# One-hot matrices of a table look-up: a compare per chunk of table rows with one row number per partition, in place of one compare of two tensors per piece

## The reference

```python
e = jnp.stack([tbl_0[ids[:, 0]], ..., tbl_26[ids[:, 26]]], axis=1)      # [2048, 27, 128]
dot_products = jnp.einsum('bnd,bmd->bnm', e, e)
z = dot_products[:, c, r]                                               # r, c = np.tril_indices(27, k=-1)
h = jnp.concatenate([z.reshape(2048, -1), dense_ctx], axis=1)           # 351 + 16
h = jnp.maximum(h @ W_top1 + b_top1, 0.0)                               # 512
h = jnp.maximum(h @ W_top2 + b_top2, 0.0)                               # 256
y = h @ W_top3                                                          # 1
```

## Time and profile before

| | us |
|---|---|
| median of 3 executions | 354.51 (354.46 to 360.79) |
| the profiled execution, its own time | 354.21 |
| span that its trace covers | 352.1 |
| TensorE busy | 330.7 (94%) |
| VectorE busy | 250.9 (71%) |
| GpSimd busy | 244.4 (69%) |
| ScalarE busy | 148.8 (42%) |

### The profile page before, as it was taken

One profiled execution on the slowest core, in us unless ns is written; L12 is line 12 of the kernel. 1 busy time (PEld: TensorE's weight loads), 2 busy tenths in 40 slices (PEclk: granted clock), 3 DMA queues, 4 the chain that ended last, 5 costly groups with the idle time before them and its releaser, 6 DMA issues.

```text
span 352.1 us, 12745 instructions
## 1 busy us (share of the span) xinstructions
PE 330.7 (94%) x5664; PEld 278.9 (79%) x5664; DVE 250.9 (71%) x335; ACT 148.8 (42%) x304; POOL 244.4 (69%) x265
## 2 busy tenths in 40 slices
PE   1897879999999999999999999999999999999986
PEld 0686768888888888888888888888888888887775
DVE  3899999989839696587929698487938786420322
ACT  2256543443534254433644245442545246535321
POOL 5777776777777777777777777777777777777100
PEclk9999999999999999999999999999999999999999
DMA  7997574443433433243332433243342332222000
GB/s 219 323 270 244 128 217 104 99 116 92 122 85 90 108 85 103 55 119 85 90 94 77 107 99 80 77 114 85 89 98 59 83 95 71 57 57 59 20 4 3
DMA packets 21928, 36.81 MB, mean 105 GB/s; under 512 B 7907, under 2 KB 12003, under 8 KB 21874
## 3 DMA queue, kind: packets, MB, share of 16 engines
q0 software_dynamic: 8256, 16.92, 19.7%
q1 hardware_dynamic: 13474, 18.55, 18.0%
q10 hardware_dynamic: 144, 0.52, 0.4%
HBM read 35.97 MB, written 0.01 MB: 102 GB/s over the span
## 4 chain that ended last, share of the span: by engine, by line
PE 87%; DVE 8%; issue 2%; DMA 1%; ACT 1%; SPq 0%; DVEq 0%
PE e_banks L560 42%; PE g_banks L594 13%; PE w_banks L624 10%; PE e_banks L572 9%; PE w_banks L655 8%; DVE one_hot L781 5%; DVE table_lo L762 3%; PE w_banks L644 2%; DMA ids_wide<-in_ids 1%; PE w_banks L613 1%; PE w_banks L666 0%; DVE g_banks L768 0%; DVE a L829 0%; ACT et L410 0%; DVE zt L795 0%
## 5 line engine op out<-in xcount | busy, mean ns | idle before, releaser
L528 POOL DMA_INDIRECT rows<-in_tbl,idx x258 | 243.6, 944 | 82.1 <-issue 77.4
L781 DVE TENSOR_TENSOR one_hot<-ids_wide,row_no 128x1024 fp32r<-128x1024 int32 x160 | 183.9, 1216 | 25.4 <-PE e_banks L560 21.4
L560 PE MATMUL e_banks<-one_hot,table_hi 128*128 128x512 f32 (+1 forms) x448 | 151.8, 356 | 5.3 <-issue 5.1
L560 PE MATMUL e_banks<-one_hot,table_lo 128*128 128x512 f32 (+1 forms) x448 | 147.2, 345 | 0.0
L560 PEld LDWEIGHTS e_banks<-one_hot,table_hi 128*128 128x128 f32 x448 | 85.5, 191 | 18.3 <-issue 7.6
L560 PEld LDWEIGHTS e_banks<-one_hot,table_lo 128*128 128x128 f32 x448 | 85.6, 191 | 9.2
L410 ACT ACTIVATE et<-e_banks 128x256 f32<-128x256 f32 x56 | 38.9, 694 | 84.7 <-PE e_banks L560 84.5
L402 ACT ACTIVATE et<-e_banks 128x512 f32<-128x512 f32 (+1 forms) x66 | 44.0, 668 | 51.5 <-PE e_banks L572 50.3
L795 DVE STREAM_TRANSPOSE zt<-g_banks 128x352 f32<-128x352 f32 (+1 forms) x32 | 17.8, 595 | 53.2 <-PE g_banks L594 53.2
L594 PEld LDWEIGHTS g_banks<-et 128*26 128x26 f32 x4096 | 42.0, 103 | 16.9 <-issue 13.2
L594 PE MATMUL g_banks<-et 128*26 128x26 f32 x4096 | 49.8, 191 | 1.2
(11 more groups left out here) (32 smaller groups left out, 111.1 us busy)
## 6 DMA issues: line engine op xcount, KB each, us to landing
ids_wide<-in_ids SPq DMA_DIRECT2D x31, 256.0 KB
et<-in_kept_tables SPq DMA_DIRECT2D x10, 512.0 KB, 9.9
rows<-in_tbl,idx POOLq DMA_INDIRECT x258
ids_wide<-in_ids SPq DMA_DIRECT2D x18, 128.0 KB
et<-in_kept_tables ACTq DMA_DIRECT2D x1, 512.0 KB, 3.9
a1T<-in_ids SPq DMA_DIRECT2D x4, 128.0 KB, 10.3
w<-in_w SPq DMA_DIRECT2D x2, 256.0 KB
w<-in_W_top SPq DMA_DIRECT2D x1, 512.0 KB
```

Of the source, the lines that this page charges most:

```text
L528: pool.indirect_dma_start(rows[:, k % RING, a, :], None, tables[f], bass.IndirectOffsetOnAxis(ap=idx[:, t, f:f + 1], axis=0)).then_inc(row ...
L560: last = nc.tensor.matmul(e_bank[n % E_BANKS][:, 0:UNIT * units_of((u, q))], part[:, q, c, :], hot_piece(o, piece)[:, i, :], start=(c == 0 ...
L781: nc.vector.tensor_tensor(hot_piece(o, piece), ids_place(o).unsqueeze(1).broadcast_to(shape), row_no[:, chunks[0]:chunks[-1] + 1].unsqueez ...
```

## The change

`row_no` moves from PSUM to SBUF. A piece of a one-hot is no longer one `tensor_tensor` compare, but one `tensor_scalar` compare for each of its chunks: the ids of 256 or 512 samples against one row number per partition, `row_no[:, c:c + 1]`. A narrow piece becomes four instructions of 256 columns, a wide one two of 512; over the kernel 174 instructions of 1024 columns become 448 (200 of 256, 248 of 512). The last of a piece's instructions signals `one_hot_ready`, and only the first of them waits. Rings, loads, the order of the pieces and the work of the other engines stay as they are.

```diff
+        row_no = sb("row_no", [P, OC])
...
-        row_no = psum("row_no", [P, OC])
...
-                shape = [P, len(chunks), UNIT * units_of(LOOK_UPS[o])]
-                nc.vector.tensor_tensor(
-                    hot_piece(o, piece),
-                    ids_place(o).unsqueeze(1).broadcast_to(shape),
-                    row_no[:, chunks[0]:chunks[-1] + 1].unsqueeze(2).broadcast_to(shape),
-                    ALU.is_equal).then_inc(one_hot_ready, 1)
+                for i, c in enumerate(chunks):
+                    last = nc.vector.tensor_scalar(hot_piece(o, piece)[:, i, :], ids_place(o), row_no[:, c:c + 1], None,
+                                                   ALU.is_equal)
+                last.then_inc(one_hot_ready, 1)
```

## The result

The changed kernel takes 368.9 us in the median of four runs (365.4 to 371.5), the kernel before 355.1 in the same job. The ratio is 1.034, 95% interval 1.028 to 1.041: slower, by more than the 2% that a measurement tells from no change. The forecast was 366 us, the range 349 to 376.

What follows compares the result with a forecast made beforehand. TensorE bounds the kernel from 56 us on, GpSimd's gathers close behind. 354.2 us, plus 16.5 of gather waits, less 1.1 of ring wait and 3.2 for which rows lay ready, gives 366 us; range 349 to 376.

Steps and rivals of the forecast that it cites:

- The bounds: TensorE has no room from 56 us on; GpSimd's gathers follow closely and may be late by 3.2 us in all.
- The price of a compare: VectorE's compares at double rate: 0.338 to 0.397 us for 512 columns, 0.206 to 0.265 for 256, 125 to 151 in sum.
- VectorE loses 0.06 us at a meeting: VectorE loses 0.06 us at each of a hundred meetings with a starting gather, hidden behind TensorE.
- the signs named ahead: 512-column compares 0.42 to 0.49 us, VectorE busy under 220, gathers of mean 1.0, last near 342, TensorE idling for DMA late.
- The start: The 28 pieces ahead of the last `table_lo` get 5 to 10 us shorter; worth nothing in the forecast time.
- The gathers: 100 to 121 of 258 gathers meet a compare and wait half of one on average: 14.7 to 21.2 us, taken 16.5.
- the fetch of row numbers: A starting gather fetches 128 row numbers from SBUF by a way VectorE also uses at two streams or double rate.
- the 12 us that the prediction named with it: If held gathers also waited some 115 ns past the VectorE instruction's end, the sum would be about 12 us larger.
- The sum: Third-last group's rows 16.5 us later, less 1.1 of ring wait and 3.2 lying ready: +12.2 on 354.2, so 366 us.
- Nothing lost: Rival: gathers lose nothing that counts, 0.02 us a meeting; whole kernel 349 to 352 us; chance 0.20.
- a wait for the end of a whole run of compares: Rival: GpSimd gets in only after a run of compares, over a microsecond a meeting; kernel beyond 450 us; chance 0.03.
- Single rate: Rival: VectorE's new compares run one column at a time, start 5 to 10 us longer; 354 to 366 us; chance 0.14.

Runs made afterwards that it cites:

- the plain loads: Each gather replaced by a load of a table's first 128 rows: 347.4 us on the kernel before; 347.7 and 342.3 us on the changed kernel.
- the first experiment: Kernel before with one tensor_tensor compare per chunk (448, of 256 and 512 columns), row_no still in PSUM: 363.5 us, ratio 1.026.

## Why the prediction was right, and where its steps were not

*The bounds.* TensorE behind 56 us, and GpSimd 3.2 us behind it: right. TensorE did go idle for rows as soon as the gathers grew, and a change of the start alone moved the time by less than 2%.

*The price of a compare.* Right at the upper ends. Eight wide ones in 3.25 us, the last of 0.49, give 0.394 us each (forecast 0.338 to 0.397), narrow ones 0.263 (0.206 to 0.265). So the double rate is there with an int32 input, and the 0.059 us of the second operand is paid. At these prices 248 and 200 compares are 150 us, forecast 125 to 151. The groups by shape list 170 (108.8 and 44.2, and two more of 9.9 and 7.4). By the records, some 11 of the other 20 us are holds by GpSimd: 64 compares are late by 0.17 us in the mean. Another 5 are the last compares of the runs, which last longer than the distance to a next one. The sentence that VectorE loses 0.06 us at a meeting was wrong by nearly a factor of three for each compare that is held. With these holds two of the signs named ahead came out just above their bounds: compares of 512 columns at 0.496 us in the mean (0.42 to 0.49), and VectorE busy for 220.9 us (under 220).

*The start.* "5 to 10 us off the stage that VectorE leads" failed: nothing came off. The wide pieces did save 3 us (the fourth `table_lo` ends at 22.53, before at 25.55). Then TensorE waited 1.75 us for rows of the first groups (22.91), because the gathers lay 2.7 us behind by then (1.8 us of holds, and 0.9 by which the first started later), and VectorE waited 2.05 us for TensorE in turn (24.57). From there on two narrow pieces took 2.3 to 2.5 us with the holds, as before. The sum didn't suffer by it, since it had given this gain no worth.

*The gathers.* Right, and it makes the verdict: 14.7 us in all (taken 16.5, bounds 14.7 to 21.2), 122 gathers that meet a compare, counted in the records by what ran 0.05 us after their start (forecast 100 to 121). But the sum came out of two terms that were off in opposite ways. 72 met a wide compare and lost 0.175 us in the mean, near the half compare of the forecast; 50 met a narrow one and lost 0.011, where half a compare is 0.13. The other 1.5 us were lost mostly beside line 830, which reads two operands from SBUF, and in one gather at 52.44 us. The forecast's average assumed that a gather falls anywhere in a compare. That fails for both: 36 of the narrow meetings began in the first 0.05 us of the compare, 39 of the wide ones 0.10 to 0.15 us into it. So it is luck that the wide ones come near the half. The mechanism as named, the fetch of row numbers, was too narrow, as the plain loads show. That a held gather gets in when one instruction ends was shown; that two streams hold it, too, and that a `tensor_scalar` at double rate does, each by itself. The Trainium skill, "SBUF — State Buffer", section "SBUF: two separate sides", has a held transfer wait until the VectorE instruction's end plus some 115 ns. The held plain loads agree, which end 0.12 us behind a compare. It adds nothing to the price of a gather's meeting, though, which was the rest of the compare less 0.13 us, so the 12 us that the prediction named with it did not come.

*The sum.* GpSimd's last gather was forecast near 342 and starts at 340.85; the third-last group's start was to come 12.2 us later and came 12.9. That is close by luck, as terms off in opposite ways cancel: the holds were 14.7 us for 16.5 taken, while the first gather started 0.9 us late, as it waited longer for `idx` (3.6 us in the group's row, 2.7 in the earlier trace rows), and the last completion signal added 1.3. What the sum did not have is 2.9 us of lower TensorE clock behind it: 366 became 369.

*The rivals.* Nothing lost, and a wait for the end of a whole run of compares, are both out by the gathers' lengths. The second of them came true for three of the 258 plain loads, so it is not excluded for every transfer. Single rate is out by 0.394 us; what it would have cost was seen in the first experiment, 363.5 us.

## What to carry to other kernels

Before you make a VectorE instruction faster, ask whether GpSimd issues transfers and has no slack. Here two streams in SBUF, or a `tensor_scalar` at the double rate within it, made a gather that began beside them wait for the running instruction, and a gather that came first held VectorE by some 0.2 us. Plain loads were tried beside the double rate only, and waited too. An operand in PSUM is worth keeping for that, even if the instruction is slower by it; moving one of 8 columns to SBUF cost 66 us here. Where two engines hold each other up at regular distances, don't average over phases: work out where the next start falls, with the holds in it.

## What the runs showed that I had not expected

- Shortening a compare from 512 to 256 columns takes the gathers' wait from 0.175 us to almost nothing rather than to half, and moves the cost to VectorE (some 0.2 us a gather, so that a piece took it 9.86 / 8 = 1.23 us where an old one took 9.13 / 8 = 1.14).
- The granted clock of TensorE falls in the last 30 us of the changed kernel (0.72 from 335 to 340, 0.89 from 360 to 368), which costs 2.9 us; the same part of the kernel before was at 1.00. TensorE had been idle for rows shortly before in this kernel. But with narrow compares from piece 28 on it fell at the end too (0.82 from 350 us on), without a wait for rows, so what brings it about stays open.
- Three plain loads that began beside narrow compares waited until the whole run of compares was over, 1.1 to 3.3 us, while gathers beside narrow compares lost 0.011 us. What lets the compares go first each time there is not shown.
- With the start alone changed, TensorE stood still for 2.3 us near 57.5 us with "issue" as the only reason, and nothing at the end moved. Three more profiles have such a stop of 2.4 to 2.8 us behind the first products, all with new compares in the whole start (`row_no` in PSUM, plain loads, compares of 256 columns); the changed kernel's has none. What it was, no run here tells.
